# Layer norms applied on ScalarE instead of VectorE, with the quantisation two steps later

## What is computed

```python
def _layernorm(x, eps=1e-05):
    m = jnp.mean(x, axis=-1, keepdims=True)
    v = jnp.var(x, axis=-1, keepdims=True)
    return (x - m) / jnp.sqrt(v + eps)

x = x + 0.5 * _ffn(_layernorm(x), ...)
x = x + _attn(_layernorm(x), ...)
x = x + 0.5 * _ffn(_layernorm(x), ...)
x = x + 0.5 * _mix(_layernorm(x), ...)
x = x + _mamba(_layernorm(x), ...)
x = x + 0.5 * _mix(_layernorm(x), ...)
```

## Time and profile before

| | |
|---|---|
| median of 3 runs | 2720.51 us (2718.44 to 2722.49) |
| profiled execution | 2725.65 us, its span 2723.8 us |
| busy share of the span | PE 94%, DVE 78%, ACT 68%, POOL 27% |
| granted TensorE clock, mean | 0.976 of full speed |

### The profile page before, as it was taken

How to read it: one execution, slowest core, us unless ns; L and a number is a source line. 1 busy time by engine, 2 the same in 40 slices (tenths; PEclk the granted TensorE clock), 3 DMA queues, 4 the chain that set the end, 5 groups by cost and what they waited for, 6 DMA issues and landing times.

```text
span 2723.8 us, 51202 instructions
## 1 busy us (share of the span) xinstructions
PE 2556.2 (94%) x17437; PEld 1698.5 (62%) x17437; DVE 2135.7 (78%) x3151; ACT 1854.0 (68%) x4430; POOL 740.4 (27%) x564
## 2 busy tenths in 40 slices
PE   5699998999999999999899999999999999999997
PEld 3557675665666656566565666656566665666665
DVE  7588776989799798879987998797788879775552
ACT  3366755867688677867767877686687768766663
POOL 1000000544055125504440452264045215400000
PEclk9799999999999999999999999999999999999997
DMA  3425353664566546556573755556466564645434
GB/s 138 139 72 139 94 150 98 162 174 120 150 151 180 129 134 175 139 153 163 133 183 88 198 151 142 162 152 170 111 186 162 148 160 132 189 102 149 113 80 93
DMA packets 753406, 385.77 MB, mean 142 GB/s; under 512 B 421568, under 2 KB 678656, under 8 KB 752768
## 3 DMA queue, kind: packets, MB, share of 16 engines
q1 hardware_dynamic: 747104, 380.66, 52.5%
q10 hardware_dynamic: 6048, 1.84, 0.3%
HBM read 274.91 MB, written 115.87 MB: 143 GB/s over the span
## 4 chain that ended last, share of the span: by engine, by line
PE 65%; DVE 17%; issue 7%; DMA 4%; ACT 3%; SPq 2%; POOL 2%; ACTq 0%; DVEq 0%; POOLq 0%
PE ps L717 14%; PE ps L739 13%; PE ps L726 12%; PE ps L786 7%; PE ps L706 7%; DVE h_ring L1226 5%; PE ps L792 4%; DVE h_nmax L1048 3%; PE ps L799 2%; SPq L515 2%; DVE h_ring L1236 1%; DMA v_d<-h_v_mixed 1%; PE ps L758 1%; POOL h_ring L653 1%; PE ps L826 1%
## 5 line engine op out<-in xcount | busy, mean ns | idle before, releaser
L893 ACT ACTIVATE h_prob<-ps,h_nmax 128x512 f32<-128x512 f32 x1024 | 709.7, 695 | 96.5 <-DVE h_nmax L1048 94.6
L1048 DVE TENSOR_REDUCE h_nmax<-ps 128x2 f32<-128x1024 f32 x512 | 621.6, 1214 | 117.0 <-PE ps L717 116.0
L726 PE MATMUL ps<-ident,h_prob 128*128 128x128 f32 x4096 | 620.8, 279 | 23.4 <-DVE h_probT L1288 13.3
L726 PEld LDWEIGHTS ps<-ident,h_prob 128*128 128x128 f32 x4096 | 479.3, 144 | 193.5 <-issue 115.2
L717 PE MATMUL ps<-h_qk 64*128 64x512 f32 x2048 | 585.5, 649 | 1.4 <-ACT h_prob L893 1.2
L1013 ACT ACTIVATE h_probT<-ps 128x512 f32<-128x512 f32 x796 | 478.0, 600 | 61.7 <-PE ps L726 59.3
L662 POOL TENSOR_TENSOR h_wide_c<-h_wide_c,h_ring 128x512 f32<-128x512 f32 x240 | 333.3, 1389 | 678.6 <-DVE h_ring L1236 678.6
L739 PE MATMUL ps<-h_probT,h_v_sb 128*64 128x256 f32 x4096 | 502.4, 388 | 6.0 <-DMA h_v_sb<-v_d 4.2
L739 PEld LDWEIGHTS ps<-h_probT,h_v_sb 128*64 128x64 f32 x4096 | 273.2, 137 | 312.8 <-issue 149.5
L1226 DVE TENSOR_TENSOR_SCAN h_ring<-h_ring 128x512 f32<-128x512 f32 x256 | 406.5, 1588 | 39.3 <-POOL h_ring L653 24.9
L653 POOL TENSOR_TENSOR h_ring<-h_m_xpad,h_m_b_rows 128x512 f32<-128x512 f32 x256 | 351.0, 1381 | 263.1 <-DVE h_m_xpad L1347 251.5
(11 more groups left out here) (215 smaller groups left out, 2597.7 us busy)
## 6 DMA issues: line engine op xcount, KB each, us to landing
h_mix_diag<-mix_blocks SPq DMA_DIRECT2D x128, 512.0 KB, 4.1
v_d<-h_v_mixed SPq DMA_DIRECT2D x128, 256.0 KB, 4.3
h_v_sb<-v_d SPq DMA_DIRECT2D x128, 256.0 KB, 3.3
at_d<-h_att SPq DMA_DIRECT2D x128, 256.0 KB, 3.1
h_mo_diag<-mo_blocks SPq DMA_DIRECT2D x128, 256.0 KB, 3.5
h_att<-at_d SPq DMA_DIRECT2D x128, 256.0 KB, 3.7
h_m_b_rows<-dbl_d SPq DMA_DIRECT2D x128, 256.0 KB, 4.5
h_m_c_rows<-dbl_d SPq DMA_DIRECT2D x128, 256.0 KB, 4.5
```

The costliest lines, as they stand in the source:

```text
L726: ins = pe.transpose(ps[:, TB + v % 2, k * P:(k + 1) * P], prob[:, v % NB, k * P:(k + 1) * P], ident[:, :])
L893: act.activation(prob[:, v % NB, :], ps[:, SB + v % 4, :], ACT.Exp, bias=nmax[:, p, j, o:o + 1], accum_out=den[:, p, j, o:o + 1]).then_inc ...
L1048: dve.tensor_reduce(nmax[:, p, j, :], ps[:, SB + 2 * w % 4:SB + 2 * w % 4 + 2, :], X, ALU.max, negate=True).then_inc(sem("row_max"), 1)
```

## The change

DVE keeps the statistics, and in part 2 makes one offset per token, minus mean times reciprocal deviation (`shift`, one instruction over 128x4). ACT multiplies by the reciprocal deviation and adds the offset, one activation per block of tokens, in the same step. The first and third norm of a front signal `f_scaled`, for which DVE waits before it quantises, and the quantisation stands two local steps later. Nothing else is changed; PE, POOL and SP have the same instructions in the same order as before.

```diff
@@ layer_norm, part 2
             else:
                 dve.wait_ge(sem(tag + "_rstd"), k + 1)
-                for j in range(J):
-                    ins = dve.tensor_scalar(bufs["nrm"][:, j, :], xb[:, j, :], mv[:, j, 0:1], bufs["rstd"][:, j:j + 1],
-                                            ALU.subtract, ALU.mult)
-                if done is None:
-                    link(ins)
-                else:
-                    ins.then_inc(done, 1)
+                dve.scalar_tensor_tensor(out=bufs["shift"][:, :], in0=mv[:, :, 0], scalar=-1.0, in1=bufs["rstd"][:, :],
+                                         op0=ALU.mult, op1=ALU.mult).then_inc(sem(tag + "_shift"), 1)
+
+        def layer_norm_apply(act, xb, k, tag, bufs, done):
+
+            act.wait_ge(sem(tag + "_shift"), k + 1)
+            for j in range(J):
+                ins = act.activation(bufs["nrm"][:, j, :], xb[:, j, :], ACT.Identity, bias=bufs["shift"][:, j:j + 1],
+                                     scale=bufs["rstd"][:, j:j + 1])
+            ins.then_inc(done, 1)
...
-        F_QUANT_AT = [[9 + i // 2 for i in range(QUANT_PARTS)], [52 + i // 2 for i in range(QUANT_PARTS)]]
+        F_QUANT_AT = [[11 + i // 2 for i in range(QUANT_PARTS)], [54 + i // 2 for i in range(QUANT_PARTS)]]
@@ ACT's loop
                             if kind == "front":
                                 o, m = front_set(n)
                                 fb = fbs[o]
+                                for k in range(3):
+                                    if u == F_NORM_AT[k][2]:
+                                        layer_norm_apply(act, fb["x"], 3 * m + k, f"f{o}_ln", fb,
+                                                         sem(f"f_normed{o}" if k == 1 else f"f_scaled{o}"))
...
                             elif kind == "prep":
+                                if u == NORM_AT[2]:
+                                    if n >= 1:
+                                        wait_full(act, "norm", 0, n - 1)
+                                    layer_norm_apply(act, x_prep if n else fbs[0]["x"], n, "ln", ln, sem("normed"))
...
                             elif kind == "mamba":
+                                if u == M_NORM_AT[2]:
+                                    layer_norm_apply(act, mb["x"][:, n % 2], n, "m_ln", mb, sem("m_normed"))
@@ DVE's loop
                                 if u == F_QUANT_AT[k][i]:
+                                    if i == 0:
+                                        dve.wait_ge(sem(f"f_scaled{o}"), 2 * m + k + 1)
                                     quantise_part(dve, link, linked, fb["nrm"].rearrange("p j (n b) -> p (j n) b", b=QBLOCK),
                                                   fb, i, sem(f"quantised{o}"))
```

More of the change, by code:

```diff
@@ L107, in macaron_kernel @@
         ln = {"stats": sb("stats", [P, J, 6]), "mv": sb("mv", [P, J, 2]), "var_e": sb("var_e", [P, J]),
-              "rstd": sb("rstd", [P, J]), "nrm": sb("nrm", [P, J, D])}
+              "rstd": sb("rstd", [P, J]), "shift": sb("shift", [P, J]), "nrm": sb("nrm", [P, J, D])}
         nrm = ln["nrm"]
@@ L123, in links, with layer_norm @@
             return link, linked
-        def layer_norm(dve, link, linked, xb, k, tag, bufs, part, done=None):
+        def layer_norm(dve, link, linked, xb, k, tag, bufs, part):
             stats, mv = bufs["stats"], bufs["mv"]
@@ L381, in macaron_kernel @@
                 for name, shape in (("stats", [P, J, 6]), ("mv", [P, J, 2]), ("var_e", [P, J]), ("rstd", [P, J]),
-                                    ("sc", [P, J * NQ]), ("rs", [P, J * NQ]), ("nmax", [P, J]), ("den", [P, J]),
+                                    ("sc", [P, J * NQ]), ("rs", [P, J * NQ]), ("shift", [P, J]), ("nmax", [P, J]), ("den", [P, J]),
                                     ("rden", [P, J])):
@@ L387, in macaron_kernel @@
                                 ("xpad", [P, HALVES, CONV - 1 + S]), ("b_rows", [P, 2, S]), ("c_rows", [P, 2, S]),
-                                ("stats", [P, J, 6]), ("mv", [P, J, 2]), ("var_e", [P, J]), ("rstd", [P, J])):
+                                ("stats", [P, J, 6]), ("mv", [P, J, 2]), ("var_e", [P, J]), ("rstd", [P, J]),
+                                ("shift", [P, J])):
                 mb[name] = t("m_" + name, shape)
@@ L1160, in front_step @@
                                     wait_taken(dve, "f_att", 0, n)
-                                layer_norm(dve, link, linked, x_, 3 * m + k, f"f{o}_ln", fb, F_NORM_AT[k].index(u),
-                                           done=sem(f"f_normed{o}") if k == 1 else None)
+                                layer_norm(dve, link, linked, x_, 3 * m + k, f"f{o}_ln", fb, F_NORM_AT[k].index(u))
                         for k in range(2):
@@ L1302, in _ @@
                                         dve.wait_ge(sem("x_prep_in"), 16 * n)
-                                if u == NORM_AT[2] and n >= 1:
-                                    wait_full(dve, "norm", 0, n - 1)
                                 if u in NORM_AT:
-                                    layer_norm(dve, link, linked, x_prep if n else fbs[0]["x"], n, "ln", ln, NORM_AT.index(u), done=sem("normed"))
+                                    layer_norm(dve, link, linked, x_prep if n else fbs[0]["x"], n, "ln", ln, NORM_AT.index(u))
                                 if u == TOP_AT[0]:
@@ L1327, in _ @@
                                 if u in M_NORM_AT:
-                                    layer_norm(dve, link, linked, mb["x"][:, n % 2], n, "m_ln", mb, M_NORM_AT.index(u),
-                                               done=sem("m_normed"))
+                                    layer_norm(dve, link, linked, mb["x"][:, n % 2], n, "m_ln", mb, M_NORM_AT.index(u))
                                 if u == CONV_AT:
```

## The result

The changed kernel took 2778.2 us (median; 2772.2 to 2786.4) against 2719.6 us for the kernel before on the same chip: a ratio of 1.020, 95% interval 1.018 to 1.022, slower by 54 us (48 to 61). The two medians themselves lie 58.6 us apart, which is inside that interval. The forecast was 2735 with a range of 2716 to 2754. The direction was right, the size was not: the time lies 24 us above the range.

The account below looks back on a forecast made before the run. Dependent steps were taken to bound the first 125 us, then a nearly full PE with some waits on DVE. Median 2720.5 plus 14.7 for the start plus 0 for the heads gave 2735 us, range 2716 to 2754.

Parts of the forecast that it names:

- What bounds the kernel: Whole kernel: dependent steps set the first 125 us; then PE is nearly full, DVE can give back at most some 45 us.
- What leaves DVE and comes to ACT: All 48 norms: DVE gives up 66.2 us and gains 8 for offsets; ACT gains some 83, 1.7 per group of four.
- The start: First fronts and first mixture norm, before the heads: four delays on the path summing to 14.7 us.
- its first step: First norm of front 0: scaling waits behind ACT's weight prologue, moving the residual add of line 1077 by +10.5 us.
- Nothing takes the shift back: Behind the start: DMAs and a PE without gaps, so first heads and the end come later by the whole shift.
- The quantisation: Heads: moving it two steps later costs nothing, as none of PE's listed waits names it.
- The coupling: Heads: ACT waits for DVE's offset and evicts attT late; 7 to 14 us in all.
- seven tight norms: Heads: norms where PE waits for the normalised rows; the coupling costs 1 to 2 us at each.
- disappear in its idle quarter: Norms behind 125 us: in an even stretch ACT's 1.7 us per group cost nothing.
- The relief: Heads: DVE is 17% of the chain, 463 us, and 2.7% less of it saves 12.5 us.
- the heads' term: Behind the start: coupling and relief called even, 0 us, with 12 to either side.
- coupling bites: Rival: ACT's waits cost PE at tight norms and fronts, relief stays off the path; +14.7 + 15, 2750; chance 0.18.

Follow-up runs that it names:

- e6: Kernel before, quantisation at its old steps, only the seven norms of the start scaled by ScalarE: ratio 1.0038, +10 us.
- e14: Kernel before, quantisation at its old steps, only the 41 norms behind the start scaled by ScalarE: ratio 1.0064, +17 us.
- e12: Kernel before, VectorE still scaling; at each norm ScalarE waits for the offset and runs five activations on constants: ratio 1.010, +27 us.
- e1: Changed kernel with the quantisation put back at its old steps: ratio 1.013, +35 us against the kernel before.
- e13: Kernel before, one VectorE instruction over 128x512 replacing the four of line 142 in the 41 norms behind the start: ratio 0.9957, -12 us.
- e8: Kernel before, VectorE still scaling and also making the offset; ScalarE only waits for it at each norm: ratio 1.0026, +7 us.
- e9: Kernel before, only each front's first quantisation moved two steps later, VectorE scaling: ratio 1.002, +5 us.

## Why the prediction was wrong, point by point

- *What bounds the kernel* was read right: PE, with stops of which DVE's part could be won back only where PE stands.
- *What leaves DVE and comes to ACT*: the group 1.64 us for 1.7, the offset 0.15 to 0.16 us in the median for 0.17, no further table load; the sums came within 10 us. Right.
- *The start*, 14.7 us: right in mechanism and 2 us too high against this trace (12.6 at 128 us); its first step gave 9.4 for 10.5. In e6, 10 us of it reach the end (6 to 15). "Nothing takes the shift back" was too strict.
- *The quantisation, "I cost at nothing: none of PE's waits of rows 3 names it, so it had room"*: this step failed, and costs 17 us (11 to 23). It asked who waits for the quantisation. The price is paid by those who stand behind it on DVE: the moved parts pushed the head output and a probability copy back, and some of these parts took twice as long beside GpSimd. The rows for this were at hand, DVE busy 439 of 500 us and PE's waits for h_att and h_probT.
- *The coupling, 7 to 14 us for seven tight norms*: the mechanism and its size at the place of the earlier trace rows are confirmed to 0.1 us. As a sum it was mis-sized. The forecast counted the seven tight places and gave the fronts' 24 norms nothing, since ACT's 1.7 us "disappear in its idle quarter". They don't: load alone costs 12.5 us, wait and load together 27 without any relief. For the fronts' later 18 norms 5 to 9 us net stand in the runs, not clear of noise.
- *The relief, 12.5 us*: it is near the 10 us between e14 and e12 and above the 2 us by e1 less e6, so its size inside the change stays open. Its price per microsecond was too low: e13 gave 12 us for under half of the time that the change takes from DVE. Where the sum agrees with a run, that is in part luck. Net the heads' term is +17 (e14) where the forecast had 0 with 12 to either side.
- *The rival "coupling bites"* (+15 for the heads) came nearest, and its +15 is near e14's +17. Its way there was not right in all: it kept relief off the path, and e13 shows relief to be worth 12 us. Had it been the forecast, with the quantisation's 17 us, the sum would have been 2720.5 + 14.7 + 15 + 17 = 2767, still 11 below the measured 2778.
- *The clock* stood in no step. Of the 47.4 us lost behind the start 22.1 are slower PE work. Each term of a stop's length has to be taken with what follows it.

The parts measured alone, start 10, later norms 17, quantisation 17, add up to 45 of the 54 us. e1, with start and later norms together, is +35 where the parts give 28. Whether these 7 to 9 us are an interaction or the sum of the intervals (each 5 us or so to either side) stays open. None of the fourteen kernels has an edit that should change nothing, so it is not known either how much of an effect of 5 to 7 us, as in e8 or e9, comes with any other placement of the same work.

## What to carry to other kernels

Before moving a step by two places because "nobody waits for it", ask who stands behind it in its new place on that engine, and read the engine's row there for gaps. Work handed to an engine that runs ahead of the giver costs the wait plus the work for everything behind it in the queue; a low mean busy share of that engine isn't cover for it. And price a stop of TensorE with the clock that follows it: here, behind the start, the lost clock nearly doubled the bill (22.1 us on top of 25.3).

## What the runs showed of the hardware

In these traces the granted clock is at half only at stops of PE or just behind them. Over the traces of all sixteen kernels, from 150 to 2450 us each, there are 248 stretches at 0.50. Each begins inside a stop or at most 2.4 us behind its end, and the longest stop there took 0.9 us or more. Of the stops of 3 us or more, 99 of 106 were followed by one, of those of 1 to 1.5 us 28 of 205. The stretches lasted 3.4 us (173 of them) or 6.8 us (75). The kernel before has 12 between 150 and 2450 us, 54.6 us in all, the changed one 21, 105.8 us; leaving out where PE stands in them, half of the rest is lost work, 26.6 and 49.0 us. The difference of 22.4 us agrees with the 22.1 us by which its PE is busy longer. e9, whose idle time behind the start equals that of the kernel before (108.4 and 108.1 us), has 17 such stretches, and its trace is 9.4 us longer all the same (its profiled execution was the slowest of its runs; the kernel itself is +5).

An activation 128x128 from SBUF with a factor and an offset per partition:

```profile
L148 ACT ACTIVATE nrm<-h_x_prep,shift,rstd x60: 477/481/496, 156.0 to 2488.2; 128x128 f32<-128x128 f32 x60
```

All 192 took 477 to 522 ns, while line 142 on DVE ran from 315 to 1317 ns.
